# A two-layer graph network on one core: the second layer as (A x1) W in transposed sums of four row blocks

## The chip, the cores and the metric

The kernel runs on one core of one Trainium2 chip. The metric is the device time of one execution in microseconds (us). Three executions of the kernel before took 679.08, 679.48 and 680.87 us, median 679.48.

## The reference

`x` is 4096 x 128 in float32, `adj` (A) is a 4096 x 4096 matrix of zeros and ones, `W` is 128 x 128. Cut to what matters:

```python
dis = clip(adj.sum(axis=1), 1.0) ** -0.5
diffusion = (dis[:, None] * adj * dis[None, :]) @ x - x
attn = softmax(beta * cosine(x, x) * adj, axis=1)
x1 = layernorm(x + diffusion + sigmoid(alpha) * (attn @ x - x))
x2 = layernorm(x1 + relu(adj @ (x1 @ W)))        # the second layer
```

## The kernel before

**Tiling.** The 4096 rows are 32 row blocks of 128 (R = 32). A row block r is the rows with one remainder modulo 4 (K = 4) within 512 rows, so four row blocks make one stretch of 512 rows of the output (b = 0 to 7). Every engine has its own program, written out by hand, in the order in which it stands there; semaphores tie the engines together. No planner sets an order.

**First part, to about 442 us: attention.** For each row block the scores, the softmax and the attention product are computed. On the way A is packed: four byte matrices are folded into one word array and turned on TensorE, so that `packT` (128 x 32 x 256 words) holds all of A transposed, four bits to a byte. Nothing of the change lies here but two tiny VectorE instructions on constants (L754, L755).

**Second part: the sums of layer 1, A times y.** For each row block, VectorE unpacks its column of A out of `packT` into one of four `stage` buffers (`stage_block`, L765, four pieces of 128 x 256 words: a shift and a mask that leave each byte as an fp8 0 or 2). TensorE then does 32 matmuls (`whole_row`, L1124, through `add_tile`, L1109), one for each block t of 128 input rows: the stationary side is the 128 x 128 fp8 tile of `stage`, whose elements lie four bytes apart, and the moving side is `y_parts[t]`, 256 columns of float16 (a high and a low part, 128 columns each, which together carry nearly float32). The 256 sums land in one bank of `ps_e`. VectorE adds both halves to `u` (`head0`, L860), takes the moments (`spread`, L853), ScalarE takes the root (`root`, L560) and VectorE normalises (`normalise`, L880) into `x1_now`.

**x1 W, in the same loop, four rows late.** In the middle of each row's 32 matmuls TensorE transposes x1 of row block r - 4 (`turn_x1`, L1114), ScalarE copies it out of PSUM and keeps x1 in `u` (`turned_out`, L564), and after the row TensorE multiplies it by W in float32 (`x1_w`, L1119). ScalarE and VectorE split the product into a high and a low float16 part in `x_parts` (`xw_high`, L571; `xw_low`, L892).

**Third part: the sums of layer 2, A times (x1 W).** The same 32 matmuls for each row block, now with `x_parts[t]` as the moving side. The first four row blocks are written out (`first_tiles`, `last_tiles`, L1150 to L1173), because the last four x1 W are not ready at their start: their transposes and products stand between the first matmuls. The other 28 row blocks are a loop of four (L1174). For each row block ScalarE takes the high half (`sum_high`, L594), VectorE adds the low one, applies relu and adds x1 (`head1`, L870), takes moments and normalises. SyncE stores four row blocks at a time (L278); the last four leave in two pieces, three row blocks and one (L281).

**Queues.** All DMAs of the late parts are SyncE's: the output stores. GpSimd has no work after about 430 us.

The program prints the functions that the diff touches:

Of the kernel before, what the change touches and what calls it, by code (L numbers as in the profile page):

```python
# [26 lines left out]
ALU = mybir.AluOpType  # L27
ACT = mybir.ActivationFunctionType
AX = mybir.AxisListType
F32 = mybir.dt.float32  # L30
# [7 lines left out]
K = 4  # L38
# [6 lines left out]
W_SCALE = 128.0  # L45
# [5 lines left out]
def two_layer_gnn(nc, x, adj, alpha, beta, weights, out):  # L51
# [17 lines left out]
    with ExitStack() as ctx:  # L69
# [35 lines left out]
        stats = sb("stats", [P, 6], F32)  # L105
        mv = sb("mv", [P, 2, 2], F32)
# [6 lines left out]
        attn_scale, x_up, dif_scale, w_up, w_down, eps_c = (c(n) for n in range(10, 16))  # L113
# [3 lines left out]
        std = col[:, 22:24]  # L117
        sign_beta, top = c(24), c(25)
        table_loads = [c(26), c(27), c(28)]
        rstd = sb("rstd", [P, 2], F32)  # L120
# [19 lines left out]
        hi_scaled = sem("hi_scaled")  # L140
# [52 lines left out]
        x1_turned = sem("x1_turned")  # L193
        x1_kept = sem("x1_kept")
        out_done = sem("out_done")
        x1t_done = sem("x1t_done")
        xw_done = sem("xw_done")
        xw_hi = sem("xw_hi")
        xw_lo = sem("xw_lo")
# [10 lines left out]
        x1t = late[:, 0:2 * P].rearrange("p (a d) -> p a d", d=P)  # L210
        x1_now = late[:, 2 * P:6 * P].rearrange("p (a d) -> p a d", d=P)
        wts = late[:, 6 * P:7 * P]
        summed = late[:, 7 * P:9 * P].rearrange("p (a d) -> p a d", d=P)
        early = scores[:, 1, :]
        xw_ps = [ps_acc, ps_at]
# [4 lines left out]
        mean = [mv[:, q, 0:1] for q in range(2)]  # L220
        var = [mv[:, q, 1:2] for q in range(2)]
        words = [adj_bytes[:, q, :].bitcast(U32).rearrange("p (i w) -> p i w", i=C) for q in range(2)]
        packed_f = [packed[:, q, :].bitcast(F32) for q in range(2)]
        stage8 = [stage[:, n, :].bitcast(F8).rearrange("p (b i k) -> p b i k", b=B, k=K) for n in range(G)]
# [8 lines left out]
        def _(sp):  # L233
# [45 lines left out]
            for part, r in ((slice(0, 3 * D), R - 1), (slice(3 * D, 4 * D), R)):  # L279
                sp.wait_ge(out_done, r)  # L280
                sp.dma_start(out_v[B - 1, :, part], u_b[:, B - 1, part]).then_inc(out_stored, 16)  # L281
# [140 lines left out]
        def _(act):  # L422
# [137 lines left out]
            def root(r, q, base):  # L560
                act.wait_ge(var_done, r + (base + 1))
                nc.scalar.activation(std[:, q:q + 1], var[q], ACT.Sqrt, bias=eps_c).then_inc(std_done, 1)  # L562

            def turned_out(r, n):  # L564

                act.wait_ge(x1_done, r + 1)
                nc.scalar.activation(u[:, r, :], x1_now[:, n, :], ACT.Copy).then_inc(x1_kept, 1)
                act.wait_ge(x1_turned, r + 1)
                nc.scalar.activation(x1t[:, n % 2, :], ps_s[:, n % 2, 0:P], ACT.Copy).then_inc(x1t_done, 1)

            def xw_high(r, n):  # L571
                act.wait_ge(xw_done, r + 1)
                nc.scalar.activation(x_parts[:, r, 0:D], xw_ps[n % 2][:, 0:P], ACT.Copy,
                                     scale=w_up).then_inc(xw_hi, 1)


            def step(r, n, lag):
                if lag >= 5:
                    xw_high(r - 5, (n + 3) % G)
                if lag >= 4:  # L580
                    turned_out(r - 4, n)
                root(r, n % 2, 0)
            for r in range(2 * G):
                step(r, r % G, r)
            with act.Fori(2 * G, R - G + 1, G) as r:
                for n in range(G):
                    step(r + n, n, 5)
            for r in range(R - G, R):
                xw_high(r - 1, (r - 1) % G)
                turned_out(r, r % G)  # L590
            xw_high(R - 1, (R - 1) % G)


            def sum_high(r, n):  # L594
                act.wait_ge(rows_done, r + (R + 1))
                nc.scalar.activation(summed[:, n % 2, :], ps_e[:, n, 0:D], ACT.Copy, scale=w_down).then_inc(hi_scaled, 1)  # L596
            sum_high(0, 0)
            for r in range(1, G):
                sum_high(r, r)
                root(r - 1, (r - 1) % 2, R)  # L600
            with act.Fori(G, R - G + 1, G) as r:
                for n in range(G):
                    sum_high(r + n, n)
                    root(r + (n - 1), (n + 1) % 2, R)
            root(R - 1, 1, R)

        @block.vector
        def _(dve):
# [10 lines left out]
            nc.vector.memset(top, 0.0).then_inc(xw_lo, 2)  # L619
# [134 lines left out]
            link(nc.vector.tensor_scalar(w_up, rpow2[:, 1:2], W_SCALE, None, ALU.mult))  # L754
            link(nc.vector.tensor_scalar(w_down, pow2[:, 1:2], 1.0 / (W_SCALE * BYTE_F8), None, ALU.mult))  # L755
# [9 lines left out]
            def stage_block(r, n, pieces=range(C)):  # L765
                for i in pieces:
                    nc.vector.tensor_scalar(stage[:, bass.ds(n, 1), i * CH // K:(i + 1) * CH // K], packT[:, bass.ds(r, 1), :], i,  # L767
                                            BYTE_ONE * 0x01010101, ALU.logical_shift_left,
                                            ALU.bitwise_and).then_inc(staged, 1)
# [83 lines left out]
            def spread(r, q, base):  # L853

                dve.wait_ge(relu_done if base else sums_read, r + 1)
                nc.vector.bn_stats(stats[:, :], u[:, r, :]).wait_op(sign_done, 1, "sem-ge").then_inc(bn_done, 1)
                dve.wait_ge(bn_done, r + (base + 1))
                nc.vector.bn_aggr(mv[:, q, :], stats[:, :]).wait_op(sign_done, 1, "sem-ge").then_inc(var_done, 1)  # L858

            def head0(r, n, first=False):  # L860
# [7 lines left out]
                spread(r, n % 2, 0)  # L868

            def head1(r, n):  # L870

                dve.wait_ge(hi_scaled, r + 1)
                nc.vector.scalar_tensor_tensor(summed[:, n % 2, :], ps_e[:, n, D:2 * D], w_down, summed[:, n % 2, :],
                                               ALU.mult, ALU.add).then_inc(sums_read, 1)
                dve.wait_ge(sums_read, r + (R + 1))
                nc.vector.scalar_tensor_tensor(u[:, r, :], summed[:, n % 2, :], 0.0, u[:, r, :],
                                               ALU.max, ALU.add).then_inc(relu_done, 1)
                spread(r, n % 2, R)

            def normalise(r, n, base, wait=True):  # L880
                q = n % 2
                dve.wait_ge(std_done, r + (base + 1))
                nc.vector.reciprocal(rstd[:, q:q + 1], std[:, q:q + 1]).then_inc(rstd_done, 1)
                dve.wait_ge(rstd_done, r + (base + 1))
                if base == 0 and wait:
                    dve.wait_ge(x1_turned, r - 3)
                    dve.wait_ge(x1_kept, r - 3)
                nc.vector.tensor_scalar(x1_now[:, n, :] if base == 0 else u[:, r, :], u[:, r, :],
                                        mean[q], rstd[:, q:q + 1], ALU.subtract,
                                        ALU.mult).then_inc(x1_done if base == 0 else out_done, 1)  # L890

            def xw_low(r, n):  # L892
                dve.wait_ge(xw_hi, r + 1)
                nc.vector.scalar_tensor_tensor(x_parts[:, r, D:2 * D], xw_ps[n % 2][:, 0:P], w_up,
                                               x_parts[:, r, 0:D], ALU.mult, ALU.subtract).then_inc(xw_lo, 1)


            def step(r, n, lag, ahead):
                dve.wait_ge(rows_done, r + 1)
                stage_block(ahead, n)  # L900
                head0(r, n, lag < G)
                if lag >= 5:
                    xw_low(r - 5, (n + 3) % G)
                if lag >= 1:
                    normalise(r - 1, (n + 3) % G, 0, lag >= 5)
            for r in range(2 * G):
                step(r, r % G, r, r + G)
            with dve.Fori(2 * G, R - 2 * G + 1, G) as r:
                for n in range(G):
                    step(r + n, n, 5, r + (n + G))  # L910
            for r in range(R - G, R):
                step(r, r % G, 5, r + G - R)
            normalise(R - 1, (R - 1) % G, 0)
            for r in range(R - 5, R):
                xw_low(r, r % G)


            dve.wait_ge(x1_kept, R)

            def last_step(r, n, more=True, stage_next=True):  # L920
                dve.wait_ge(rows_done, r + (R + 1))
                if stage_next:
                    stage_block(r + G, n)
                head1(r, n)
                if more:
                    normalise(r - 1, (n + 3) % G, R)
            for r in range(G):
                last_step(r, r, r >= 1)
            with dve.Fori(G, R - 2 * G + 1, G) as r:
                for n in range(G):  # L930
                    last_step(r + n, n)
# [267 lines left out]
```

## Time and profile before

| | |
|---|---|
| median of three executions | 679.48 us |
| the profiled execution, its own time | 679.01 us |
| its span, first to last instruction | 677.2 us |
[...]
| TensorE busy | 652.0 us (96%) |
| VectorE busy | 561.9 us (83%) |
| ScalarE busy | 436.2 us (64%) |
| GpSimd busy | 245.5 us (36%) |
| sums of layer 1 with row blocks 4 to 31 | 449.7 to 557.7 us |
| sums of layer 2 | 557.7 to 672.4 us |
| after the last matmul | 672.4 to 677.2 us |

A busy share is the time in which an engine had an instruction in hand. Matmuls overlap: one takes longer from its start to its end than the distance to the next one's start, so the rate of TensorE is read from that distance, and the mean duration in a group's row is not the price of one more.

### The profile page before, as it was taken

How to read it: one execution, taken by the hardware profiler on the slowest of the kernel's cores; microseconds unless marked ns; L12 is line 12 of the kernel's file. 1: busy time of each engine (PE TensorE's matmuls, PEld its weight loads, DVE VectorE, ACT ScalarE, POOL GpSimd, SP SyncE). 2: the span in 40 equal slices, each digit the busy share in tenths (PEclk: the TensorE clock that was granted, in tenths of full speed). 3: DMA queues.
4: the chain of work that ended last, by engine and by line, in shares of the span. 5: the costliest groups of instructions: out<-in, count | busy, mean ns of one | idle time of the engine just before them, and what ended most of it. 6: DMA issues, size and time to landing. Idle time of an engine off the chain costs nothing.

```text
span 677.2 us, 17913 instructions
## 1 busy us (share of the span) xinstructions
PE 652.0 (96%) x5623; PEld 517.4 (76%) x5623; DVE 561.9 (83%) x1678; ACT 436.2 (64%) x885; POOL 245.5 (36%) x229
## 2 busy tenths in 40 slices
PE   6679999999999999999999999899999999999997
PEld 6347777777777777777777776799888888888886
DVE  4879999999999999999999999767767766666664
ACT  5989998998999999989999988512222223111111
POOL 2899446455455464454464557300000000000000
PEclk8999999999999999999999999999999999999999
DMA  6589999999999999999999994300000000000000
GB/s 252 187 222 237 256 264 239 256 255 237 263 257 248 250 255 251 247 266 248 254 247 256 261 234 81 67 1 1 0 0 0 0 0 1 17 15 31 15 15 31
DMA packets 154538, 105.30 MB, mean 155 GB/s; under 512 B 135696, under 2 KB 136208, under 8 KB 154512
## 3 DMA queue, kind: packets, MB, share of 16 engines
q1 hardware_dynamic: 154080, 104.94, 61.1%
q8 instruction: 10, 0.16, 0.1%
q14 instruction: 16, 0.13, 0.1%
q10 hardware_dynamic: 432, 0.07, 0.1%
HBM read 69.34 MB, written 2.10 MB: 105 GB/s over the span
## 4 chain that ended last, share of the span: by engine, by line
PE 85%; DVE 5%; DMA 3%; POOL 3%; ACT 2%; SPq 1%; issue 1%; ACTq 0%; DVEq 0%; POOLq 0%
PE ps_e L1111 31%; PE ps_s L981 21%; PE ps_e L1013 8%; PE ps_e L992 7%; PE ps_acc L1013 7%; PE ps_e L1016 4%; PE ps_acc L1016 3%; DMA eTx<-e_parts 2%; DVE e_parts L717 2%; DMA col<-in_L_gnn_beta 1%; PE ps_e L1030 1%; DVE scores L696 1%; PE ps_at L965 1%; POOL x_parts L341 1%; PE ps_s L1030 1%
## 5 line engine op out<-in xcount | busy, mean ns | idle before, releaser
L981 PE MATMUL ps_s<-xn_parts,xn_signed 128*128 128x512 f16 x756 | 203.7, 379 | 5.5 <-DVE cmax L696 5.5
L696 DVE CUSTOM_DVE_ANT_1 scores<-ps_s,adj_bytes 128x512 f32<-128x512 f32 x252 | 171.4, 682 | 16.9 <-PE ps_s L981 9.3
L502 ACT ACTIVATE scores<-scores,col 128x1024 f32<-128x1024 f32 x128 | 157.4, 1232 | 4.5 <-DVE col L707 4.3
L326 POOL TENSOR_SCALAR e_parts<-scores 128x1024 f16<-128x1024 f32 x64 | 80.4, 1256 | 157.3 <-ACT scores L502 84.7
L448 ACT ACTIVATE adj_bytes<-land 128x1024 uint8<-128x1024 f32 x128 | 133.5, 1047 | 1.6 <-POOL packed L318 1.6
L1111 PE MATMUL ps_e<-x_parts,stage 128*128 128x256 f16 x1024 | 113.0, 273 | 0.0
L1111 PEld LDWEIGHTS ps_e<-x_parts,stage 128*128 128x128 fp8e4 x1024 | 100.2, 98 | 11.5
L1111 PE MATMUL ps_e<-y_parts,stage 128*128 128x256 f16 x896 | 105.4, 273 | 0.2
L981 PEld LDWEIGHTS ps_s<-xn_parts,xn_signed 128*128 128x128 f16 x756 | 69.5, 98 | 41.7 <-DVE cmax L696 5.5
L717 DVE SCALAR_TENSOR_TENSOR e_parts<-scores,e_parts 128x1024 f16<-128x1024 f32 x64 | 97.5, 1524 | 0.5 <-POOL e_parts L326 0.4
L509 ACT ACTIVATE eT_parts<-ps_e 128x512 f16<-128x512 f32 x128 | 75.7, 591 | 32.0 <-PE ps_e L992 31.4
L1111 PEld LDWEIGHTS ps_e<-y_parts,stage 128*128 128x128 fp8e4 x896 | 87.3, 98 | 10.5 <-issue 1.0
L767 DVE TENSOR_SCALAR stage<-packT 128x256 uint32 (+1 forms) x256 | 58.2, 288 | 40.8 <-PE ps_e L1111 40.8
L711 DVE SCALAR_TENSOR_TENSOR eT_parts<-ps_e,eT_parts 128x512 f16<-128x512 f32 x128 | 87.5, 683 | 1.5 <-ACT eT_parts L509 1.5
L562 ACT ACTIVATE col<-mv,col 128x1 f32<-128x1 f32 x64 | 18.6, 290 | 101.3 <-DVE mv L858 101.3
L992 PE MATMUL ps_e<-ident,scores 128*128 128x128 f32 x512 | 77.8, 274 | 0.4 <-ACT scores L502 0.4
L596 ACT ACTIVATE scores<-ps_e,col 128x128 f32<-128x128 f32 x32 | 11.8, 369 | 88.0 <-PE ps_e L1111 88.0
L992 PEld LDWEIGHTS ps_e<-ident,scores 128*128 128x128 f32 x512 | 53.9, 141 | 2.9 <-ACT scores L502 0.9
L1013 PE MATMUL ps_e<-x_parts,eT_parts 128*128 128x256 f16 x256 | 49.2, 273 | 2.2 <-DVE eT_parts L711 2.1
L1013 PE MATMUL ps_acc<-x_parts,eTx 128*128 128x256 f16 x256 | 49.2, 273 | 1.8 <-DMA eTx<-e_parts 1.7
L1013 PE MATMUL ps_acc<-x_parts,eT_parts 128*128 128x256 f16 x256 | 49.2, 273 | 1.0 <-DVE eT_parts L711 1.0
L1013 PE MATMUL ps_e<-x_parts,eTx 128*128 128x256 f16 x256 | 49.2, 273 | 0.0
(132 smaller groups left out, 992.2 us busy)
## 6 DMA issues: line engine op xcount, KB each, us to landing
land<-in_adj SPq DMA_DIRECT2D x128, 512.0 KB, 4.7
x_keep<-in_x SPq DMA_DIRECT2D x4, 512.0 KB, 8.6
out<-u SPq DMA_DIRECT2D x7, 256.0 KB, 2.0
eTx<-e_parts SPq DMA_TRANSPOSE x64, 5.1
out<-u SPq DMA_DIRECT2D x1, 192.0 KB, 1.9
eT_parts<-in_L_gnn_weights ACTq DMA_DIRECT2D x1, 64.0 KB, 8.7
scores<-in_L_gnn_weights SPq DMA_DIRECT2D x1, 64.0 KB, 2.5
out<-u SPq DMA_DIRECT2D x1, 64.0 KB, 1.6
```

Source lines behind the costliest of these rows:

```text
L326: nc.gpsimd.tensor_scalar(e_parts[:, n, 0, :], scores[:, q, (n + 2) * CH:(n + 3) * CH], E_SCALE, 1.0, ALU.mult, ALU.mult).wait_op(sign_don ...
L448: nc.scalar.activation(adj_bytes[:, q, i * CH:(i + 1) * CH], land[:, i, :], ACT.Copy, scale=float(BYTE_ONE >> i), accum_out=deg[:, i, bass ...
L502: nc.scalar.activation(piece, piece, ACT.Exp, bias=neg_max[q], scale=abs_beta, accum_out=csum[:, q, i:i + 1]).then_inc(exp_done, 1)
L509: nc.scalar.activation(eT_parts[:, b, 0, :], ps_e[:, b % 2, :], ACT.Copy, scale=E_SCALE).then_inc(e_hi, 1)
L696: nc.vector.tensor_tensor_reduce(scores[:, q, o:o + BANK].rearrange("p (k q) -> p k q", k=K), score_bank(h, r == 0 if start else False).re ...
L711: nc.vector.scalar_tensor_tensor(eT_parts[:, b, 1, :], ps_e[:, b % 2, :], E_SCALE, eT_parts[:, b, 0, :], ALU.mult, ALU.subtract).then_inc( ...
L717: nc.vector.scalar_tensor_tensor(e_parts[:, n, 1, :], scores[:, q, (n + 2) * CH:(n + 3) * CH], E_SCALE, e_parts[:, n, 0, :], ALU.mult, ALU ...
L767: nc.vector.tensor_scalar(stage[:, bass.ds(n, 1), i * CH // K:(i + 1) * CH // K], packT[:, bass.ds(r, 1), :], i, BYTE_ONE * 0x01010101, AL ...
L981: ins = nc.tensor.matmul(score_bank(h, start), xn_signed[:, q, part, :], xn_parts[:, other, o:o + BANK], start=(part == 0 and other == 0), ...
L992: ins = nc.tensor.transpose(ps_e[:, b % 2, n * P:(n + 1) * P], scores[:, q, t * P:(t + 1) * P], ident[:, :])
L1013: nc.tensor.matmul(attn_ps[q][:, 0:2 * D], hi, x_parts[:, t, :], start=(k == 0 and n == 0), stop=(k == H - 1 and n == TH - 1), skip_group_ ...
L1111: return nc.tensor.matmul(ps_e[:, n, 0:2 * D], lhs[:, b, :, k], y[t], start=(t == 0), stop=(t == R - 1))
```

## The change

The second layer is computed as (A x1) W instead of A (x1 W), and its sums come out transposed.

- **Layer 1** no longer transposes x1 and no longer multiplies it by W. x1 stays in `u`, and ScalarE and VectorE split x1 itself, times 256, into `x_parts` (`x1_high`, `x1_low`), one and two steps after its row.
- **Layer 2** works on quads of four row blocks (`z_rows`). For each of the 32 blocks t there are two matmuls, one for the high and one for the low part of x1: the stationary side is `x_parts[t]`, 128 x 128 float16, the moving side is 512 columns of fp8, 128 from each of four `stage` rows, with elements four bytes apart. All 64 accumulate in one bank of `ps_s`, which then holds (A x1) of 512 rows, transposed.
- ScalarE copies that bank into `zT` (`keep_z`). After the 18th matmul of the next quad TensorE multiplies the four 128-column pieces by W in float32 (`z_w`), with `zT` as the stationary side, so that the product comes out with rows on the partitions. VectorE then applies relu and adds x1 for the four row blocks in one instruction (`relu_add`).
- Quads alternate between two staging buffers: the old `stage` and the space of `land`, where A had been landing. The last quad is done in two halves of two row blocks, with 256 columns in each matmul. The last store holds two row blocks instead of one.

```diff
-            def normalise(r, n, base, wait=True):
...
+            def x1_low(r):
+                dve.wait_ge(x1_hi, r + 1)
+                nc.vector.scalar_tensor_tensor(x_parts[:, r, D:2 * D], u[:, r, :], X1_SCALE, x_parts[:, r, 0:D],
+                                               ALU.mult, ALU.subtract).then_inc(x1_lo, 1)
...
+            def relu_add(j, r, rows):
+
+                dve.wait_ge(zw_done, j + 1)
+                nc.vector.scalar_tensor_tensor(u[:, r:r + rows, :], zw_ps[j % 2][:, 0:rows * P].rearrange(
+                    "p (n d) -> p n d", d=D), 0.0, u[:, r:r + rows, :], ALU.max, ALU.add).then_inc(relu_done, 1)
+                dve.wait_ge(relu_done, j + 1)
+                for n in range(rows):
+                    nc.vector.bn_stats(stats[:, n, :], u[:, r + n, :]).then_inc(bn_done, 1)
+                for n in range(rows):
+                    dve.wait_ge(bn_done, R + r + n + 1)
+                    ins = nc.vector.bn_aggr(mv[:, n, :], stats[:, n, :])
+                ins.then_inc(var_done, 1)
...
+            for n in range(G):
+                stage_block(G + n, n)
+            for j in range(1, B):
+                relu_add(j - 1, (j - 1) * G, G)
+                if j < B - 1:
+                    dve.wait_ge(z_done, j)
+                    for n in range(G):
+                        stage_block((j + 1) * G + n, n, to=(j + 1) % 2)
+                x2_norm(j - 1, (j - 1) * G, G)
+            relu_add(B - 1, R - G, 2)
+            x2_norm(B - 1, R - G, 2)
+            relu_add(B, R - 2, 2)
+            x2_norm(B, R - 2, 2)
```

```diff
+            keep_z(0, G)
+            for j in range(1, B - 1):
+                keep_z(j, G)
+                roots(j - 1, G)
+            keep_z(B - 1, 2)
+            roots(B - 2, G)
+            keep_z(B, 2)
+            roots(B - 1, 2)
+            roots(B, 2)
```

```diff
-            def whole_row(r, n, y, layer):
...
-                    if layer == 0 and t == R // 2:
-                        turn_x1(r - G, n)
                 ins.then_inc(rows_done, 1)
-                if layer == 0:
-                    x1_w(r - G, n)
+
+            def z_w(j, q, rows, reuse=True):
+
+                pe.wait_ge(z_kept, j + 1)
+                if reuse:
+                    pe.wait_ge(relu_done, j - 1)
+                for n in range(rows):
+                    ins = nc.tensor.matmul(zw_ps[q][:, n * P:(n + 1) * P], zT[:, q, n * P:(n + 1) * P], wts,
+                                           start=True, stop=True)
+                ins.then_inc(zw_done, 1)
+
+            def z_rows(j, q, quad, n, rows, reuse=True, turn=None, first=False):
+
+                pe.wait_ge(staged, quad * (G * C) + (R * C + G * C))
+                if reuse:
+                    pe.wait_ge(z_kept, j - 1)
+                for t in range(R):
+                    b, k = t // K, t % K
+                    if first and t == 0:
+                        pe.wait_ge(x1_lo, R - G)
+                    elif first and t >= R - G:
+                        pe.wait_ge(x1_lo, t + 1)
+                    for part in range(2):
+                        ins = nc.tensor.matmul(ps_s[:, q, 0:rows * P], x_parts[:, t, part * D:(part + 1) * D],
+                                               quads8[q if rows == G else 1][:, b, k, n:n + rows, :],
+                                               start=(t == 0 and part == 0), stop=(t == R - 1 and part == 1))
...
+                    if t == R // 4 and turn:
+                        turn()
+                ins.then_inc(z_done, 1)
...
+            z_rows(0, 0, 0, 0, G, reuse=False, first=True)
+            z_rows(1, 1, 1, 0, G, reuse=False, turn=lambda: z_w(0, 0, G, reuse=False))
+            z_rows(2, 0, 2, 0, G, turn=lambda: z_w(1, 1, G, reuse=False))
+            with pe.Fori(3, B - 1, 2) as j:
+                z_rows(j, 1, j, 0, G, turn=lambda: z_w(j - 1, 0, G))
+                z_rows(j + 1, 0, j + 1, 0, G, turn=lambda: z_w(j, 1, G))
+            z_rows(B - 1, 1, B - 1, 0, 2, turn=lambda: z_w(B - 2, 0, G))
+            z_rows(B, 0, B - 1, 2, 2, turn=lambda: z_w(B - 1, 1, 2))
+            z_w(B, 0, 2)
```

TensorE, one row block of layer 1's loop, before (L1111 is a sum's matmul, L1117 the transpose of x1, L1122 its product with W; `[waits ...]` names the semaphores):

```order
L1127 REGISTER_ALU [waits staged]
L1111 MATMUL ps_e<-y_parts,stage 128x256 [waits sums_read,ident_done]
L1111 MATMUL ps_e<-y_parts,stage 128x256 x16
L1117 MATMUL ps_s<-ident,scores 128x128 [waits x1_done]
L1111 MATMUL ps_e<-y_parts,stage 128x256 x15
L1122 MATMUL ps_acc<-scores 128x128 [waits xw_lo,x1t_done]
```

and with the change, the last row block of layer 1 (L1107), a quad of layer 2 (L1135) with the products by W of the quad before (L1119), and the end of the program:

```order
L1107 MATMUL ps_e<-y_parts,stage 128x256 [waits sums_read,staged,ident_done]
L1107 MATMUL ps_e<-y_parts,stage 128x256 x31
...
L1135 MATMUL ps_s<-land,x_parts 128x512 [waits z_kept,staged,ident_done]
L1135 MATMUL ps_s<-land,x_parts 128x512 x17
L1119 MATMUL ps_at<-scores 128x128 [waits z_kept]
L1119 MATMUL ps_at<-scores 128x128 x3
L1135 MATMUL ps_s<-land,x_parts 128x512 x46
...
L1135 MATMUL ps_s<-stage,x_parts 128x256 x46
L1119 MATMUL ps_acc<-scores 128x128 [waits relu_done,z_kept]
L1119 MATMUL ps_acc<-scores 128x128
```

The transpose and the product have left layer 1's loop; the products now stand in groups of four inside layer 2, and the last two behind all sums.

VectorE in layer 2, with the change: what it does between two quads (L897 is relu_add, L901 and L904 the moments, L758 the staging of the quad after next, L909 and L912 the normalising):

```order
L897 SCALAR_TENSOR_TENSOR u<-ps_acc,u 128x512 [waits zw_done]
L901 BN_STATS stats<-u 128x6 [waits relu_done]
L901 BN_STATS stats<-u 128x6 x3
L904 BN_AGGR mv<-stats 128x2 [waits bn_done] x4
L758 TENSOR_SCALAR land<-packT 128x256 [waits z_done]
L758 TENSOR_SCALAR land<-packT 128x256 x15
L909 RECIPROCAL rstd<-std 128x4 [waits std_done]
L912 TENSOR_SCALAR u<-u,mv,rstd 128x128 [waits rstd_done]
L912 TENSOR_SCALAR u<-u,mv,rstd 128x128 x3
```

Before, the staging of one row block (four pieces) stood ahead of each row's own additions; now sixteen pieces stand in one piece of the program, behind the relu and the moments of the quad before.

## Rows read from the trace of the kernel before

**Rows 1.** The page, section 4: the chain that ended last.

```profile
PE 85%; DVE 5%; DMA 3%; POOL 3%; ACT 2%; SPq 1%; issue 1%; ACTq 0%; DVEq 0%; POOLq 0%
PE ps_e L1111 31%; PE ps_s L981 21%; PE ps_e L1013 8%; PE ps_e L992 7%; PE ps_acc L1013 7%; PE ps_e L1016 4%; PE ps_acc L1016 3%; DMA eTx<-e_parts 2%; DVE e_parts L717 2%; DMA col<-in_L_gnn_beta 1%; PE ps_e L1030 1%; DVE scores L696 1%; PE ps_at L965 1%; POOL x_parts L341 1%; PE ps_s L1030 1%
```

**Rows 2.** The chain in order of time (start, us, what), layers 1 and 2.

```profile
449.73 1.85 PE ps_e L1111 x17
451.58 0.11 PE ps_s L1117
451.69 1.64 PE ps_e L1111 x15
453.33 0.22 PE ps_acc L1122 x2
453.55 1.86 PE ps_e L1111 x17
...
511.39 0.03 issue
511.42 2.02 PE ps_e L1111 x17
...
557.71 0.02 issue
...
565.51 106.89 PE ps_e L1111 x979
672.40 0.02 issue
```

**Rows 3.** Windows: us, busy us of each engine, clock, DMA share, GB/s.

```profile
435.40:557.70 122.30, 122.10 (x1121) 109.80 (x1119) 84.59 (x344) 26.90 (x114) 0.00 (x0) 1.00 0.00 0
565.34:672.40 107.06, 107.04 (x981) 95.69 (x978) 69.56 (x297) 17.45 (x62) 0.00 (x0) 1.00 0.05 18
```

**Rows 4.** The page, section 5: matmuls of 512 columns, three to a group.

```profile
L981 PE MATMUL ps_s<-xn_parts,xn_signed 128*128 128x512 f16 x756 | 203.7, 379 | 5.5 <-DVE cmax L696 5.5
```

**Rows 5.** Timeline of TensorE, attention part (start, duration, instruction).

```profile
302.46 0.61 PE L992 MATMUL ps_e<-ident,scores 128*128 128x128 f32 x4
302.91 0.81 PE L981 MATMUL ps_s<-xn_parts,xn_signed 128*128 128x512 f16 x3
303.56 0.27 PE L1013 MATMUL ps_acc<-x_parts,eTx 128*128 128x256 f16 x1
303.67 0.22 PE L1016 MATMUL ps_acc<-x_parts,eTx 128*128 128x128 f16 x1
...
304.16 0.22 PE L1016 MATMUL ps_acc<-x_parts,eTx 128*128 128x128 f16 x1
304.22 0.38 PE L981 MATMUL ps_s<-xn_parts,xn_signed 128*128 128x512 f16 x1
```

**Rows 6.** Groups by shape: loads of the stationary side.

```profile
L1111 PEld LDWEIGHTS ps_e<-x_parts,stage 128*128 128x128 fp8e4 x977 | 95.6, 98 | 11.1
L981 PEld LDWEIGHTS ps_s<-xn_parts,xn_signed 128*128 128x128 f16 x753 | 69.2, 98 | 41.5 <-DVE cmax L696 5.5 <-DVE xn_parts L646 1.7 <-issue 1.6
```

**Rows 7.** Timeline of VectorE, one step of layer 1, and the next step's start.

```profile
511.33 0.90 DVE L767 TENSOR_SCALAR stage<-packT 128x256 uint32 x4 [0.71 <-PE ps_e L1111]
...
514.02 0.35 DVE L888 TENSOR_SCALAR scores<-u,mv,rstd 128x128 f32 x1
515.35 0.90 DVE L767 TENSOR_SCALAR stage<-packT 128x256 uint32 x4 [0.98 <-PE ps_e L1111]
```

**Rows 8.** The page, section 5: widths of 512 on VectorE and ScalarE.

```profile
L509 ACT ACTIVATE eT_parts<-ps_e 128x512 f16<-128x512 f32 x128 | 75.7, 591 | 32.0 <-PE ps_e L992 31.4
L711 DVE SCALAR_TENSOR_TENSOR eT_parts<-ps_e,eT_parts 128x512 f16<-128x512 f32 x128 | 87.5, 683 | 1.5 <-ACT eT_parts L509 1.5
```

**Rows 9.** Timeline of the tail, after the last matmul.

```profile
672.42 0.37 ACT L596 ACTIVATE scores<-ps_e,col 128x128 f32<-128x128 f32 x1 [2.94 <-PE ps_e L1111]
673.27 0.29 DVE L876 SCALAR_TENSOR_TENSOR u<-scores,u 128x128 f32<-128x128 f32 x1
673.67 0.29 DVE L856 BATCH_NORM_STATS2 stats<-u 128x6 f32<-128x128 f32 x1
674.07 0.18 DVE L858 BATCH_NORM_AGGREGATE mv<-stats 128x2 f32<-128x6 f32 x1
674.29 0.30 ACT L562 ACTIVATE col<-mv,col 128x1 f32<-128x1 f32 x1 [1.32 <-DVE mv L858]
674.61 0.17 DVE L883 RECIPROCAL rstd<-col 128x1 f32<-128x1 f32 x1
674.82 0.35 DVE L888 TENSOR_SCALAR u<-u,mv,rstd 128x128 f32<-128x128 f32 x1
```

**Rows 10.** Timeline of TensorE, seam of the layers: a product with W after a wait.

```profile
560.97 0.49 PE L1122 MATMUL ps_acc<-scores 128*128 128x128 f32 x2 [1.08 <-ACT scores L569]
561.29 0.38 PE L1111 MATMUL ps_e<-x_parts,stage 128*128 128x256 f16 x2
```

**Rows 11.** The page, section 6: stores of the output, time to landing.

```profile
out<-u SPq DMA_DIRECT2D x7, 256.0 KB, 2.0
...
out<-u SPq DMA_DIRECT2D x1, 192.0 KB, 1.9
...
out<-u SPq DMA_DIRECT2D x1, 64.0 KB, 1.6
```

More of the change, by code:

```diff
@@ L44 @@
 X_SCALE = 4096.0
-W_SCALE = 128.0
+X1_SCALE = 256.0
 LN_EPS = 1e-5
@@ L112, in two_layer_gnn @@
         total, r_total, gain = (c(n) for n in range(7, 10))
-        attn_scale, x_up, dif_scale, w_up, w_down, eps_c = (c(n) for n in range(10, 16))
+        attn_scale, x_up, dif_scale, _, _, eps_c = (c(n) for n in range(10, 16))
         great = col[:, 16:18]
@@ L278, in _ @@
                 sp.dma_start(out_v[b], u_b[:, b, :]).then_inc(out_stored, 16)
-            for part, r in ((slice(0, 3 * D), R - 1), (slice(3 * D, 4 * D), R)):
+            for part, r in ((slice(0, 2 * D), R - 2), (slice(2 * D, 4 * D), R)):
                 sp.wait_ge(out_done, r)
@@ L577, in step @@
[L577 to L600, printed above, removed]
+                nc.scalar.activation(x_parts[:, r, 0:D], u[:, r, :], ACT.Copy, scale=X1_SCALE).then_inc(x1_hi, 1)
@@ L601, in _, with step, keep_z @@
+            def step(r, n, first=False):
+                root(r, n % 2)
+                if not first:
+                    x1_high(r - 1)
+            for r in range(G):
+                step(r, r, r == 0)
             with act.Fori(G, R - G + 1, G) as r:
                 for n in range(G):
-                    sum_high(r + n, n)
-                    root(r + (n - 1), (n + 1) % 2, R)
-            root(R - 1, 1, R)
+                    step(r + n, n)
+            x1_high(R - 1)
+            def keep_z(j, rows):
+                act.wait_ge(z_done, j + 1)
+                if j >= 2:
+                    act.wait_ge(zw_done, j - 1)
+                nc.scalar.activation(zT[:, j % 2, 0:rows * P], ps_s[:, j % 2, 0:rows * P], ACT.Copy,
+                                     scale=1.0 / (BYTE_F8 * X1_SCALE)).then_inc(z_kept, 1)
@@ L901, in step @@
-                head0(r, n, lag < G)
-                if lag >= 5:
-                    xw_low(r - 5, (n + 3) % G)
+                if to == 1:
+                    stage_block(ahead, n)
+                head0(r, n, first)
                 if lag >= 1:
[L905 to L926, printed above, removed]
+                    x1_norm(r - 1, (n + 1) % 2)
@@ L1020, in _ @@
             y_tiles = [y_parts[:, t, :, :] for t in range(R)]
-            xw_tiles = [x_parts[:, t, :] for t in range(R)]
             def sums(r, i):
@@ L1124, in whole_row @@
-            def whole_row(r, n, y, layer):
-                pe.wait_ge(staged, r * C + (layer * R * C + C))
-                pe.wait_ge(sums_read, r + (layer * R + 1 - G))
+            def whole_row(r, n):
+                pe.wait_ge(staged, r * C + C)
+                pe.wait_ge(sums_read, r + (1 - G))
                 for t in range(R):
-                    ins = add_tile(n, stage8[n], t, y)
+                    b, k = t // K, t % K
+                    ins = nc.tensor.matmul(ps_e[:, n, 0:2 * D], stage8[n][:, b, :, k], y_tiles[t],
+                                           start=(t == 0), stop=(t == R - 1))
```

162 lines of the change are left out of this document (57 added, 105 removed).

## The prediction

> **What bounds the kernel now.** I read the shares of the chain first: TensorE holds 85% of it, and L1111, the sums of both layers, is the largest single line with 31% [rows 1]. Then the chain in order of time, from the first row block of layer 1's loop. From 449.73 us on it is TensorE's own work without a break: 17 sums, the transpose of x1, 15 sums, the product with W [rows 2]. Layer 1's part ends at 557.71, layer 2 runs to 672.40, and its last 979 matmuls are one unbroken piece of 106.89 us, so 106.89 / 979 = 0.1092 us for one of 256 columns [rows 2]. [...] So only three things can move the time: what TensorE issues, what its instructions cost each, and the tail. All below is against the profiled execution, 679.01 us; the median of the runs, 679.48, lies 0.47 above it. A difference of 0.3%, 2 us, is about what a measurement of this kernel can tell from none.
>
> **Layer 1: what leaves.** Before, it took 557.71 - 449.73 = 107.98 us [rows 2]. Its 28 row blocks keep their 32 sums each: 28 x 32 x 0.1092 = 97.8 us. The rest, 10.2 us, is what goes. 28 transposes at 0.11 are 3.1 us and 28 products at 0.22 are 6.2 us [rows 2]; 0.9 us is left over, and it sits at the turns of the loop, where the first 17 sums take 2.02 instead of 1.85 us behind a product that waits for ScalarE [rows 2]. The changed loop has no such wait, like layer 2's loop before, which runs through its turns unbroken. I take all 10.2 us; if the turns stay, 9.3. The seam's last four transposes and products go too; they are inside layer 2's time below.
>
> Cover: VectorE's step of layer 1 takes from 511.33 to 514.37, 3.04 us, and then waits for the next row's sums [rows 7]. A row block now lasts 3.49 us instead of some 3.8, so 0.45 us of cover is left. Its instructions stay as many (the low part of x1 takes the place of the low part of x1 W), and TensorE needs a staged row three rows later. ScalarE loses two copies a row. I cost both at nothing; were VectorE 0.5 us longer a step, layer 1 would lose about that much a row.
>
> **The seam.** The first quad needs x1 parts up to row block 27 at once, which are ready two rows earlier, and the last four only at its 57th matmul, 12 us in. After the last row's sums VectorE has two additions, moments, two normalisings and three low parts to do, at 0.2 to 0.35 us each and with its waits less than a step and a half, 4.5 us. No wait. The 16 staging pieces of the second quad follow: 4 x 0.90 = 3.6 us [rows 7], done at about 8 of 13.7 us.
>
> **Layer 2: the price of a sum.** The columns are the same: 1024 x 256 before, 7 x 64 x 512 plus 128 x 256 now. No row shows a 512-column matmul with fp8 on the moving side. The nearest row is the scores' matmul, 128 x 512 in float16 with a new stationary tile each time: three take 203.7 / 252 = 0.808 us to the end of the third, which lasts 0.379, so the distance is (0.808 - 0.379) / 2 = 0.2147 us [rows 4], and the timeline has 0.65 us for three [rows 5]. That is 0.0037 us less than two of 256 columns. The float16 loads of the stationary side take 98 ns as the fp8 ones do [rows 6] and hide under 215 ns more easily than under 109.
>
> So 448 x 0.2147 = 96.2 us and 128 x 0.1092 = 14.0 us. The 32 products with W are as many as before, 30 of them between the sums: 30 x 0.22 = 6.6 us. Sum 116.8 us, against 672.40 - 557.71 = 114.7: layer 2 is 2.1 us longer on TensorE, only because the products moved into it.
>
> What the moving side's pattern costs is the unknown: single bytes, four bytes apart, in four runs of 128. Lower bound: nothing, since the stationary load of the very same bytes is as fast as a dense float16 one [rows 6]. First upper bound: each run costs as if it were a matmul of its own. Four pairs of 256 and 128 columns take 304.22 - 303.56 = 0.66 us, less 4 x 0.1092, so 128 columns alone cost 0.056 us [rows 5], and 448 x (4 x 0.0558 - 0.2147) + 128 x (2 x 0.0558 - 0.1092) = 4.1 us. Second upper bound: float32 tiles, the one case of elements four bytes apart on both sides, take (302.91 - 302.46) / 4 = 0.1125 us for 128 columns, twice the float16 price [rows 5]. I take nothing, because the load of the same tile is the nearest row.
>
> [...]
>
> [...]
>
> **Layer 2: the other engines.** A quad lasts 64 x 0.2147 + 4 x 0.22 = 14.6 us. The product with W stands behind 18 sums, 3.9 us in; ScalarE's copy of 512 columns takes some 0.6 us [rows 8], so it is there. VectorE's train starts when the products are done, 4.75 us in: relu and add 0.68 [rows 8], four times moments at 0.29 and 0.18 [rows 9], 1.9 us, staging 3.6 [rows 7], waits 0.4, together 6.6 us at most. It ends at 11.4 of 14.6 us, and the quad after next, which is what it stages, starts then. The normalising that follows waits for a root that ScalarE does only after the next copy; that is 2.3 us into the next quad at most, before VectorE is wanted at 4.75. In the two half quads nothing is staged.
>
> **The tail.** Before: 672.40 to 677.20, 4.8 us, of which 2.77 to the end of the last normalising (674.82 + 0.35) [rows 9] and 2.0 for the store. Now, from the last sum: copy of 256 columns, between 0.37 at 128 [rows 9] and 0.59 at 512 [rows 8], 0.45; two products, the first 0.49 after a wait [rows 10], 0.76 in all; meanwhile ScalarE takes the root for the half before (0.3) and VectorE normalises it (reciprocal and two, to about 1.55), and is free only then; relu and add of 256 columns, 0.42; two pairs of moments 0.9, root 0.3, reciprocal 0.15, two normalisings 0.7. The end lies at about 4.05 us, the store adds 2.2, since its 128 KB lie between 64 and 192 KB, 1.6 and 1.9 us to landing [rows 11]. 6.25 us, so 1.45 more than before; 0.8 to 2 would not surprise.
>
> **The sum.** -10.15 + 2.1 + 1.45 = -6.6 us. 679.01 - 6.6 = 672.4 for the profiled execution, 672.9 for a median. Nothing before 442 us changes but two 0.15 us instructions on VectorE while GpSimd leads; I count them at nothing.
>
> **The rivals.**
>
> 1. *The four runs cost like four matmuls.* For it: 128 columns cost 0.056 us and not 0.0537 wherever a matmul starts [rows 5]. Against: a run inside one instruction is no start. 672.9 + 4.1 = 677.0 us. Chance 0.09.
>
> 2. *The strided moving side streams at half rate*, on the other side of zero. Place: all 576 sums of layer 2. It decides once a 512-column matmul takes more than 0.2147 + 8.6 / 576 = 0.230 us, that is from 7% slower streaming on: there the change is slower than before by 2 us. At the price of the float32 rows, 448 x (0.450 - 0.2147) + 128 x (0.225 - 0.1092) = 120 us, 793 us. For it: no row shows fp8 or any stride on the moving side, and the only elements four bytes apart pay double. [...] Chance 0.08. VectorE and ScalarE would then wait.
>
> 3. *VectorE's train becomes the bound of the quads.* If it takes more than 14.6 - 4.75 = 9.85 us instead of 6.6, each of six quads starts late. With 11 us, 1.1 us a quad, 6.6 us are gone: 679.5, no difference. For it: 16 pieces in one place are a burst that did not exist. Against: a reserve of half its length. Chance 0.05.
>
> **The numbers.** The forecast has 0.78: its own ends are 671.0 (tail +0.8, matmuls at 0.2133) and 675 (turns stay, tail +2, a few tenths a quad). Rival 1 reaches 677. The range 671.0 to 677.5 holds both, 0.87, and leaves out rivals 2 and 3. Faster by over 0.3%, under 677.4 us: 0.87; within: 0.05; slower: 0.08.
>
> **What would show it.** In the changed profile: L1107 at 3.49 us a row block without breaks; L1135 with 512 columns at a distance of 0.215 us, 0.224 by rival 1, 0.45 by rival 2; a quad at 14.6 us; no wait of TensorE for VectorE's staging; 28 x 0.33 us gone from layer 1; from the last sum to the span's end 6.2 us. A distance over 0.23 us, or TensorE waiting for the staging, would make the prediction wrong.

## The result, and the profile after

The changed kernel takes 677.89 us (median of 9, 677.62 to 679.56), the kernel before 679.33 us (9 runs) beside it: a ratio of 0.9982, 95% interval 0.9974 to 0.9990. The forecast was 672.9 us, with a range of 671.0 to 677.5. The direction is right, the gain is 1.4 us instead of 6.6, and the time lies 0.4 us outside the range.

The chain in order of time (start, us, what) has the whole of layers 1 and 2 in a few pieces. L1107 is layer 1's sums, L1135 layer 2's, L1119 the products with W:

```profile
449.77 97.81 PE ps_e L1107 x896
547.59 18.52 PE ps_s L1135 x82
566.10 0.89 PE ps_acc L1119 x8
566.99 14.45 PE ps_s L1135 x64
581.45 0.89 PE ps_at L1119 x8
...
643.71 12.43 PE ps_s L1135 x64
656.14 0.89 PE ps_acc L1119 x8
657.03 7.25 PE ps_s L1135 x64
664.29 0.44 PE ps_at L1119 x4
664.73 5.23 PE ps_s L1135 x46
669.96 0.02 issue
```

Against [rows 2]: layer 1 fell from 107.98 to 97.81 us, 896 sums in one unbroken piece, 0.1092 us each; the seam costs nothing. Layer 2 rose from 114.69 to 669.96 - 547.59 = 122.37 us, where 116.8 were forecast. It has no wait in it either. A piece of 64 matmuls of 512 columns takes 14.45 us, 0.2258 each instead of 0.2147, and one of 256 columns 7.25 / 64 = 0.1133 instead of 0.1092. The windows of the same two stretches and of the tail (us, busy us of PE, PEld, DVE, ACT, POOL, clock, DMA share, GB/s) say that TensorE was busy throughout both layers, at a granted clock of 1.00 there, as in [rows 3]:

```profile
449.77:547.59 97.82, 97.82 (x898) 87.62 (x896) 73.51 (x314) 17.30 (x58) 0.00 (x0) 1.00 0.00 0
547.59:669.98 122.39, 122.36 (x636) 62.05 (x634) 48.27 (x226) 6.76 (x18) 0.00 (x0) 1.00 0.04 16
669.98:675.80 5.82, 0.71 (x4) 0.52 (x4) 2.57 (x11) 0.86 (x3) 0.00 (x0) 0.93 0.13 45
```

So the missing gain is no wait: it lies inside the matmuls. By shape, the groups of the changed kernel (busy us, mean ns) show each 512-column matmul at 387 ns from start to end, where the scores' of the same width take 379 [rows 4]; the loads of the stationary side take 96 ns, no more than the 98 of [rows 6]:

```profile
L1135 PE MATMUL ps_s<-land,x_parts 128*128 128x512 fp8e4 x256 | 59.0, 387 | 0.0
L1135 PEld LDWEIGHTS ps_s<-stage,x_parts 128*128 128x128 f16 x320 | 30.6, 96 | 26.7
L1135 PE MATMUL ps_s<-stage,x_parts 128*128 128x256 fp8e4 x128 | 15.0, 275 | 0.0
```

### The profile page after: what moved, and what is told of

The parts are those of the page before. It is cut to its first block, busy times and chain, and to the rows that moved or that the text cites. A ratio compares the mean times of both kernels' runs of the same rounds, so it can differ in the third digit from the quotient of the medians.

```text
span 675.8 us, 16373 instructions
## 1 busy us (share of the span) xinstructions
PE 652.8 (97%) x5143; PEld 470.1 (70%) x5143; DVE 534.2 (79%) x1598; ACT 414.1 (61%) x775; POOL 244.9 (36%) x229
## 4 chain that ended last, share of the span: by engine, by line
PE 85%; DVE 4%; DMA 3%; POOL 3%; ACT 2%; SPq 1%; issue 1%; DVEq 0%; ACTq 0%; POOLq 0%
PE ps_s L974 21%; PE ps_s L1135 17%; PE ps_e L1107 14%; PE ps_e L1006 8%; PE ps_e L985 7%; PE ps_acc L1006 7%; PE ps_e L1009 4%; PE ps_acc L1009 3%; DMA eTx<-e_parts 2%; DVE e_parts L710 1%; DMA col<-in_L_gnn_beta 1%; PE ps_e L1022 1%; DVE scores L689 1%; PE ps_at L958 1%; SPq L242 1%; POOL x_parts L339 1%
## 5 line engine op out<-in xcount | busy, mean ns | idle before, releaser
L324 POOL TENSOR_SCALAR e_parts<-scores 128x1024 f16<-128x1024 f32 x64 | 84.0, 1313 | 158.2 <-ACT scores L500 93.0
L1107 PE MATMUL ps_e<-y_parts,stage 128*128 128x256 f16 x896 | 98.0, 273 | 0.0
L1107 PEld LDWEIGHTS ps_e<-y_parts,stage 128*128 128x128 fp8e4 x896 | 87.7, 98 | 10.1
L583 ACT ACTIVATE scores<-ps_s 128x512 f32<-128x512 f32 (+1 forms) x9 | 4.9, 549 | 113.7 <-PE ps_s L1135 113.7
L560 ACT ACTIVATE std<-mv,col 128x1 f32<-128x1 f32 x32 | 9.4, 295 | 88.2 <-DVE mv L855 88.2
L1135 PE MATMUL ps_s<-stage,x_parts 128*128 128x512 fp8e4 (+1 forms) x320 | 59.3, 342 | 0.0
L1135 PE MATMUL ps_s<-land,x_parts 128*128 128x512 fp8e4 x256 | 59.0, 387 | 0.0
L758 DVE TENSOR_SCALAR stage<-packT 128x256 uint32<-128x256 uint32 (+1 forms) x192 | 42.6, 287 | 14.1 <-PE ps_e L1107 14.1
L1135 PEld LDWEIGHTS ps_s<-stage,x_parts 128*128 128x128 f16 x320 | 30.6, 96 | 26.7
```

Of the source, the lines that this page charges most:

```text
L324: nc.gpsimd.tensor_scalar(e_parts[:, n, 0, :], scores[:, q, (n + 2) * CH:(n + 3) * CH], E_SCALE, 1.0, ALU.mult, ALU.mult).wait_op(sign_don ...
L1107: ins = nc.tensor.matmul(ps_e[:, n, 0:2 * D], stage8[n][:, b, :, k], y_tiles[t], start=(t == 0), stop=(t == R - 1))
L1135: ins = nc.tensor.matmul(ps_s[:, q, 0:rows * P], x_parts[:, t, part * D:(part + 1) * D], quads8[q if rows == G else 1][:, b, k, n:n + rows ...
```

## The experiments

Every kernel below is the changed one with one edit, of which the lines that matter are shown ("..." marks what is left out). Line numbers shift with an edit (L1144, L1148 are then layer 2's sums, L1128, L1132 the products with W). All but the last three kernels (half words, half words with the tail's edit, the tail's edit alone) alter only what the matmuls of layer 2 stream, the first also how VectorE lays it out. Between the first and those three, every kernel streams other bytes of the staging buffers than the sums need, so its second layer has other values than the reference; the counts and widths of its matmuls and the waits in its program are those of the changed kernel. These kernels ran once each. Where layer 1 begins varies between 448.2 and 451.0 us in the profiled executions, before anything that the edits touch, so whole times can differ by that much, and the argument rests on the distances between matmuls.

### Four runs, the step, or fp8?

Three differences from the scores' matmul could make a streamed column dearer: four runs instead of one, single bytes four apart instead of elements side by side, and fp8. The first kernel lays the quad out so that all 512 bytes lie in one run, still four apart:

```diff
-quads8 = [a.bitcast(F8).rearrange("p n (b i k) -> p b k n i", b=B, k=K) for a in stages]
+quads8 = [a.rearrange("p n w -> p (n w)").bitcast(F8).rearrange("p (b m k) -> p b k m", b=B, k=K) for a in stages]
...
```

> The quad's staging buffer is laid out as (b, n, i) instead of (n, b, i), so that the 512 bytes a matmul streams lie in one run, still four bytes apart; VectorE's staging pieces write two runs of 128 words each instead of one of 256. In the changed kernel one matmul of 512 columns stands 0.2258 us from the next, 0.0111 more than the scores' 0.2147, and one of 256 columns 0.1133, 0.0041 more than layer 1's 0.1092. Theory A, the starts of further runs cost about 3.7 to 4.1 ns each (three in 512 columns, one in 256): the distance falls to 0.215 and 0.109, layer 2's sums go from 122.4 to about 116.8 us, the kernel to about 672.3 us. Theory B, the step of four bytes costs it: nothing changes, 677.9 us. Theory C, fp8 on the moving side costs it: nothing changes, 677.9 us.

Measured: 678.02 us, ratio to before 0.998 (0.9969 to 0.9990), and layer 2 exactly as before the edit:

```profile
567.60 14.45 PE ps_s L1144 x64
582.05 0.89 PE ps_at L1128 x8
```

The second keeps the four runs and puts the bytes side by side:

```diff
-quads8 = [a.bitcast(F8).rearrange("p n (b i k) -> p b k n i", b=B, k=K) for a in stages]
+quads8 = [a.bitcast(F8).rearrange("p n (b k i) -> p b k n i", b=B, k=K, i=P) for a in stages]
```

> Four runs of 128 as in the changed kernel, but bytes side by side instead of four apart. It sums other bytes of the same staging buffer in the second layer, so that layer's values are not the reference's; counts, sizes and waits are the same. Theory A (starts of runs): distance stays 0.226 us, 677.9. Theory B (step of four bytes): 0.215, 672.3. Theory C (fp8 on the moving side): 0.226, 677.9.

Measured: 672.7 us; from its chain:

```profile
547.74 17.70 PE ps_s L1135 x82
...
566.32 13.81 PE ps_s L1135 x64
580.14 0.89 PE ps_at L1119 x8
...
652.63 6.99 PE ps_s L1135 x64
...
665.10 0.02 issue
```

13.81 / 64 = 0.2158 us for 512 columns and 6.99 / 64 = 0.1092 for 256. Four runs cost nothing. The third streams float16 side by side:

```diff
-quads8 = [a.bitcast(F8).rearrange("p n (b i k) -> p b k n i", b=B, k=K) for a in stages]
+quads8 = [a.rearrange("p n w -> p (n w)").bitcast(F16).rearrange("p (t m) -> p t m", m=BANK) for a in stages]
...
-                                               quads8[q if rows == G else 1][:, b, k, n:n + rows, :],
+                                               quads8[q if rows == G else 1][:, t % 16, n * P:(n + rows) * P],
```

> The moving side reads 512 float16 values side by side in one run from the same staging buffer, the stationary side is as in the changed kernel. The second layer's values are not the reference's. Theories A, B and C: 0.215 us for 512 columns and 0.109 for 256, 672.3 us. Theory D, that the high and low part of x1 as stationary side cost it (or anything else outside the moving side): 0.226, 677.9 us.

Measured: 672.56 us, and in the chain 13.81 and 6.99 us for 64 matmuls of 512 and of 256 columns. So fp8 side by side costs what float16 does, and the high and low parts of x1 as stationary side cost nothing. The fourth doubles the number of runs and keeps the step:

```diff
-quads8 = [a.bitcast(F8).rearrange("p n (b i k) -> p b k n i", b=B, k=K) for a in stages]
+quads8 = [a.bitcast(F8).rearrange("p n (c b i k) -> p b k n c i", c=2, b=B // 2, i=P, k=K) for a in stages]
...
-                                               quads8[q if rows == G else 1][:, b, k, n:n + rows, :],
+                                               quads8[q if rows == G else 1][:, b % 4, k, n:n + rows, :, 0:P // 2],
```

> Eight runs of 64 bytes, four bytes apart, instead of four of 128 (and four of 64 in the half quads). The second layer's values are not the reference's. Theory A, 3.7 ns for each further run: 0.2147 + 7 x 0.0037 = 0.241 us for 512 columns and 0.1092 + 3 x 0.004 = 0.121 for 256, layer 2's sums 129.9 us instead of 122.4, the kernel about 685.4 us. Theories B and C: 0.226 and 0.113, 677.9 us.

Measured: 676.96 us, and again 14.45 us for 64 matmuls:

```profile
566.40 14.45 PE ps_s L1135 x64
```

Theory A falls twice: one run is no faster than four, and eight are no slower. C falls with the second kernel, D with the third. Theory B stands: the step of four bytes costs it. Layer 2's sums take 665.10 - 547.74 = 117.36 us with four dense runs, 5.0 us less than the 122.37 of the changed kernel, so the step accounts for 5.0 of the 5.6 us by which layer 2 missed its forecast.

### What a step costs

Now the step alone is varied, always in one run of 512, with k as 2, 8, 16 and 32, and once float16 at the addresses of the first experiment:

```diff
-quads8 = [a.bitcast(F8).rearrange("p n (b i k) -> p b k n i", b=B, k=K) for a in stages]
+quads8 = [a.rearrange("p n w -> p (n w)").bitcast(F8).rearrange("p (t m k) -> p t k m", m=BANK, k=2) for a in stages]
...
```

> One run of fp8 bytes two apart. The second layer's values are not the reference's here and in the next three. With bytes side by side the distance of two 512-column matmuls was 0.2158 us (13.81 / 64), with bytes four apart 0.2258. Law 1, the streaming is bound by stretches of 16 bytes, one in 0.2258 / 128 = 1.76 ns: at two apart there are 64 of them, 0.113 us, hidden, so 0.216 us and a kernel of about 672.6. Law 2, any step but one costs 5%, whatever its size: 0.226 us, 677.9.

> One run of fp8 bytes eight apart. Law 1 (1.76 ns for each stretch of 16 bytes, two elements in one): 256 x 1.76 = 0.450 us for 512 columns and 0.225 for 256, layer 2's sums 448 x 0.450 + 128 x 0.225 + 6.7 = 237 us instead of 122.4, kernel about 792 us. Law 2: 0.226 us, 677.9.

> One run of fp8 bytes sixteen apart, one element in each stretch of 16 bytes. Law 1: 512 x 1.76 = 0.90 us for 512 columns, layer 2's sums about 468 us, kernel about 1023 us. Law 2: 0.226 us, 677.9.

> The very addresses of the one-run layout, four bytes apart, but read as float16 (two bytes at each) instead of fp8. If the distance in bytes decides (law 1 and law 2 alike): 0.226 us, 677.9. If it is fp8 with a step that costs, and float16 is free of it: 0.216 us, 672.6.

> One run of fp8 bytes 32 apart; the second layer's values are not the reference's. Four, eight and sixteen apart took 0.2258, 0.452 and 0.900 us for 512 columns, in proportion to the bytes spanned. Law 1a, each stretch of 16 bytes that holds an element costs 1.76 ns: 32 apart costs no more than 16 apart, 0.90 us, kernel about 1029 us. Law 1b, the bytes that are walked over cost 0.11 ns each: 1.80 us, kernel about 1490 us.

From the chains of the five, in this order, one piece of 64 matmuls of 512 columns each:

```profile
564.63 13.81 PE ps_s L1135 x64
```

```profile
584.12 28.90 PE ps_s L1135 x64
```

```profile
622.66 57.58 PE ps_s L1135 x64
```

```profile
565.60 14.45 PE ps_s L1135 x64
```

```profile
623.16 58.72 PE ps_s L1135 x64
```

| elements | bytes apart | us for 512 columns | ns for each 16 bytes with an element | kernel, us |
|---|---|---|---|---|
| fp8, float16 | side by side | 0.2158 | (hidden) | 672.7, 672.56 |
| fp8 | 2 | 0.2158 | (hidden) | 671.1 |
| fp8 | 4 | 0.2258 | 1.76 | 677.89 |
| float16 | 4 | 0.2258 | 1.76 | 676.26 |
| fp8 | 8 | 0.4516 | 1.76 | 792.39 |
| fp8 | 16 | 0.900 | 1.76 | 1029.01 |
| fp8 | 32 | 0.9175 | 1.79 | 1036.93 |

Law 1 named 792 us for eight apart and 1023 for sixteen; 792.39 and 1029.01 were measured. The 6 us at sixteen are the products with W: the granted clock falls from 1.00 to 0.50 in that kernel, and 30 of them take 7.5 x 1.71 = 12.8 us in place of 6.7. Law 2, a fixed surcharge for any step, fails at both ends: two apart is free (0.2158 us), eight apart doubles the time (0.4516). The run with 32 bytes separates a price for each 16 bytes with an element from a price for the bytes walked over: from 16 to 32 apart the time for 512 columns rises by 2%, from 0.900 to 0.9175 us, and not by 100%. Float16 at the fp8 addresses costs the same, 0.2258 us, so the element's size has no part in it there. The streamed side behaves as if it were fed in stretches of 16 bytes, one in 1.76 ns. Only side by side and steps of 2, 4, 8, 16 and 32 bytes were run, and why the last costs 1.79 ns is open. A column side by side costs (0.2158 - 0.1092) / 256 = 0.4164 ns, so four take 1.67 ns: with four elements in a stretch the feed is 5% too slow, with eight it is hidden.

A rival to this law is TensorE's clock. From eight to sixteen apart the distance doubles, and in the kernel with 16 apart the granted clock falls from 1.00 to 0.50. Two windows of that kernel decide it. Each goes from the start of one matmul of 512 columns to the start of the fourth after it (the counts take in those that reach over the ends), the first before the fall and the second after it:

```profile
547.87:551.47 3.60, 3.60 (x6) 0.47 (x5) 3.14 (x16) 0.92 (x3) 0.00 (x0) 1.00 0.00 0
553.27:556.87 3.60, 3.60 (x6) 0.51 (x5) 0.32 (x2) 0.00 (x0) 0.00 (x0) 0.50 0.00 0
```

Four distances are 3.60 us at either clock, 0.90 each, so the clock has no part in that price.

### The remedy that follows, and the tail

By this law the bytes need only be two apart. VectorE can unpack half words for that instead of words: the mask keeps one bit of each byte, so a shift within half a word leaves the same bits, and low and high halves go to separate places. Quad 0, which is staged between layer 1's steps, keeps the old layout.

```diff
...
+                for i in range(C):
+                    for h in range(2):
+                        ins = nc.vector.tensor_scalar(
+                            halves[to][:, 2 * i:2 * i + 2, h, n, :],
+                            packT[:, r, :].bitcast(U16).rearrange("p (b i h) -> p b h i", b=2, h=2)[:, :, h, :], i,
+                            BYTE_ONE * 0x0101, ALU.logical_shift_left, ALU.bitwise_and)
...
```

> The remedy that law 1 gives. VectorE unpacks quads 1 to 7 not as words but as half words, low and high halves to separate places, so that the bytes a matmul streams stand two apart; 512 elements a piece instead of 256. Quad 0 stays four apart. Law 1: quads 1 to 6 run at 0.216 us a matmul, the half quads at 0.109, layer 2's sums take 14.45 + 82.9 + 14.0 + 6.7 = 118.0 us instead of 122.4, the kernel about 673.5 us. Against it: the staging may double, from 3.3 to 6.6 us a quad (0.204 us for 256 elements), and VectorE's train then ends 13.2 us into a quad of 14.7; if 512 half words cost more than 0.5 us a piece, TensorE waits for the staging and part or all of the 4.4 us is lost again.

Measured: 673.34 us (5 runs, 672.47 to 673.94), with the kernel before at 679.08 beside it: ratio 0.9912, interval 0.9898 to 0.9925. The first piece holds quad 0 with 64 matmuls four bytes apart, and 18 of quad 1; all later ones are at 0.2158:

```profile
546.81 18.34 PE ps_s L1148 x82
565.15 0.89 PE ps_acc L1132 x8
566.04 13.81 PE ps_s L1148 x64
...
652.35 6.99 PE ps_s L1148 x64
```

Layer 2 takes 664.82 - 546.81 = 118.01 us, the 118.0 of the expectation. VectorE's timeline (start, us, instruction) between two products with W shows the price on the other side:

```profile
566.08 0.69 DVE L910 SCALAR_TENSOR_TENSOR u<-ps_acc,u 128x512 f32<-128x512 f32 x1 [9.59 <-PE ps_acc L1132]
566.80 0.87 DVE L914 BATCH_NORM_STATS2 stats<-u 128x6 f32<-128x128 f32 x4
567.59 0.36 DVE L917 BATCH_NORM_AGGREGATE mv<-stats 128x2 f32<-128x6 f32 x4
567.87 6.52 DVE L769 TENSOR_SCALAR land<-packT 128x256 uint16<-128x256 uint16 x32
```

The staging takes 6.52 us instead of 3.29 and is done at 574.39. Quad 1 began at 546.81 + 64 x 0.2258 = 561.26 and lasts 14.7 us, to 575.97: 1.6 us of reserve are left.

One more edit concerns the tail. ScalarE takes the root of the first half quad before it copies the last sums, with half words and, in a second kernel, without them:

> As the kernel with half words, and ScalarE takes the root of the first half quad before it copies the last sums, so that VectorE has normalised that half before the tail. In the changed kernel VectorE is busy with it until 671.30, 1.34 us after the last sum, while the last products with W are there some 1.15 us after it. Expected: the tail is 0.2 to 0.3 us shorter than with half words alone, below what the times can tell but plain in the trace.

> The changed kernel with only the root's place moved as said before. Expected: from the last sum to the span's end 5.82 us becomes 5.5 to 5.6, all else as in the changed kernel; 677.6 us.

```diff
             roots(B - 2, G)
-            keep_z(B, 2)
             roots(B - 1, 2)
+            keep_z(B, 2)
             roots(B, 2)
```

Measured: 673.72 us (5 runs, 672.28 to 673.86) with half words and 678.7 us (one run) without. By the traces the time from the last sum to the span's end went from 670.6 - 664.82 = 5.78 to 670.4 - 664.72 = 5.68 us, and from 675.8 - 669.96 = 5.84 to 676.9 - 671.24 = 5.66. So 0.1 to 0.2 us, half of what was expected. In the changed kernel VectorE reached the last relu at 671.30, 1.34 us after the last sum (first line). Freed, it still waits for the products until 665.93 - 664.72 = 1.21 us after it (half words with the tail's edit, the other three lines), so only 0.13 us was there to gain:

```profile
671.30 0.42 DVE L897 SCALAR_TENSOR_TENSOR u<-ps_acc,u 128x256 f32<-128x256 f32 x1
...
664.74 0.38 ACT L586 ACTIVATE scores<-ps_s 128x256 f32<-128x256 f32 x1 [3.53 <-PE ps_s L1148]
665.18 0.71 PE L1132 MATMUL ps_acc<-scores 128*128 128x128 f32 x4 [0.47 <-ACT scores L586]
665.93 0.43 DVE L910 SCALAR_TENSOR_TENSOR u<-ps_acc,u 128x256 f32<-128x256 f32 x1 [3.88 <-PE ps_acc L1132]
```

No run's time can tell the tail's edit from none.

## Why the prediction was right, and where it was wrong

| term | forecast | measured |
|---|---|---|
| layer 1 | -10.15 | 97.81 - 107.98 = -10.17 |
| layer 2 on TensorE | +2.1 | 122.37 - 114.69 = +7.7 |
| tail | +1.45 | 5.84 - 4.80 = +1.0 |
| sum | -6.6 | -1.4 (span 677.2 to 675.8) |

**Layer 1.** Right in every part: the transposes, the products and the turns of the loop. The turns vanished with the wait that stood in them, as forecast. VectorE stayed hidden; its wait for the next row's sums is 0.47 and 0.63 us in two steps where 0.45 was forecast:

```profile
512.82 0.90 DVE L758 TENSOR_SCALAR stage<-packT 128x256 uint32 x4 [0.47 <-PE ps_e L1107]
...
516.31 0.90 DVE L758 TENSOR_SCALAR stage<-packT 128x256 uint32 x4 [0.63 <-PE ps_e L1107]
```

**Seam and other engines.** Right. In the changed kernel the staging of a quad began after relu and moments at 568.82 and took 3.29 us, far from the bound; rival 3 did not occur.

```profile
568.82 3.29 DVE L758 TENSOR_SCALAR land<-packT 128x256 uint32<-128x256 uint32 x16
```

**Layer 2's price.** This is the step that failed, in the prediction's words: of what the moving side's pattern costs, "I take nothing, because the load of the same tile is the nearest row." The runs put 5.0 us in its place, 448 x (0.2258 - 0.2158) + 128 x (0.1133 - 0.1092), and the step of four bytes is what costs it. The load of the stationary side takes 98 ns [rows 6]. Its 128 bytes four apart are 32 stretches of 16, and if they were fed as the streamed ones are, that would be 32 x 1.76 = 56 ns, an estimate: a load of 98 ns could not have shown the limit, whichever way it is fed. Another 0.5 us is the distance read from [rows 4]: side by side the matmuls stand 0.2158 apart, not 0.2147. The mean duration of a merged group gives the distance only to a nanosecond or so, and 448 of them count. The chain of the kernel before has three of the scores' matmuls at 0.65 us, which 3 x 0.2158 = 0.647 gives and 3 x 0.2147 = 0.644 does not; a long piece such as 13.81 / 64 tells the two apart with certainty. Together 5.5 of the 5.6 us by which layer 2 missed.

**The rivals.** Rival 1 came within a microsecond of the time by the wrong mechanism: runs cost nothing, and the kernel with one run gained nothing. The price it put on the sum, 4.1 us, was near the true one by luck. Its sign was a distance of 0.224 us, and 0.2258 was measured: that sign alone could not tell it from a strided side that streams a little slower, which only the experiments did. Rival 2 had the mechanism, the strided moving side, with the price of the float32 rows; the distance stayed under the 0.230 us from which it was to decide. The second upper bound, twice the time, is what eight apart costs (0.4516 us), but nothing links the float32 rows to that. For four apart it was 0.22 us for 512 columns too high, and the prediction had no price between it and zero but rival 1's. The range ended half a microsecond above rival 1, and 0.4 us short of the measured time. Nor was a distance over 0.23 us a good sign of being wrong: at 0.2258 most of the gain was gone. The forecast's own lower end adds up to 672.9 - 0.65 - 0.6 = 671.6 us and not 671.0; nothing rests on it.

Counted by the elements that share 16 bytes of the streamed side, two take 0.4516 us for 512 columns, 2.1 times the 0.2158 of side by side, four take 0.2258, 5% more, and eight 0.2158: the price of a stretch, 1.76 ns here, is hidden where eight elements share it.

**The tail.** Right in its order; the forecast was 0.4 us too long, because two like instructions on VectorE, one behind the other, take less than twice the time of one. Two normalisings take 0.60 us (673.02 in the changed kernel's timeline) where one takes 0.35 [rows 9] and 0.7 was summed, and they stand there twice. The moments of two row blocks take 672.49 - 671.75 = 0.74 us with their waits where 0.9 was summed. The store took 2.2 us as forecast.

## What to carry to other kernels

When a change swaps the sides of a matmul, price the new moving side by its own pattern: count how many elements of a streamed run fall into 16 bytes, and expect what these runs showed for steps of 4, 8 and 16 bytes, 1.76 ns for each such stretch, unless the columns themselves take longer (0.2158 us for 512 of them at a granted clock of 1.00). A load of the same bytes as stationary side said nothing about it here: it took 98 ns, as the dense float16 one did [rows 6]. When a gain is missing and no wait has appeared, divide the longest unbroken piece by its count before anything else; here one division, 14.45 / 64, showed where the gain was lost; why it was lost took the experiments.

## What the runs showed of the hardware

- The streamed side of a matmul behaves as if it were fed in stretches of 16 bytes, one in 1.76 ns (1.79 at 32 bytes apart), for the steps that were run: for 512 columns two bytes apart take the 0.2158 us of side by side, four apart 0.2258 (5% more), eight apart 0.4516 (2.1 times), sixteen apart 0.900 (4.2 times), 32 apart 0.9175 (2% above sixteen). At four apart it does not depend on the element's size (fp8 or float16), and not on the number of runs (one, four or eight): 64 matmuls take 14.45 us in each of these kernels.
- The feed's rate did not follow TensorE's granted clock. A stretch took 0.4516 / 256 = 1.76 ns at eight apart, with a granted clock of 1.00 through layer 2, and 0.900 / 512 = 1.76 ns at sixteen apart, where the granted clock fell from 1.00 to 0.50, although the matmuls stood without a gap; they took 0.90 us each before and after the fall. The windows of the kernel with 16 apart, in layer 1 and in layer 2:

```profile
450.00:547.00 97.00, 97.00 (x891) 86.88 (x890) 72.74 (x311) 16.92 (x56) 0.00 (x0) 1.00 0.00 0
550.00:700.00 150.00, 150.00 (x180) 24.08 (x179) 14.91 (x72) 1.42 (x4) 0.00 (x0) 0.51 0.01 2
```

- The four products with W of a quad follow the granted clock: in the same kernel, at 0.50, they take 1.71 us instead of the 0.89 at 1.00.
- VectorE's shift and mask took as long per element on uint16 elements read four bytes apart as on uint32 side by side: 6.52 us for 32 x 256 against 3.29 for 16 x 256.
